# An edge sort moved out of its own stage into a slot pipeline with the convolution, and edge counts made two columns at a time

## The reference

```python
x = x + _L0_conv_ref(_ln_c(x), ...)
t = _to_tokens(x)
t = t + _L0_ffn_ref(_ln_t(t), ...)                 # routed experts
x = _from_tokens(t, x)
x = x + _L1_conv_ref(_ln_c(x), L1_conv_weight, L1_conv_bias)   # relu(conv3x3 + bias)
t = _to_tokens(x)
t = t + _L1_ffn_ref(_ln_t(t), ..., L1_ffn_edge_index)
...
# in _L1_ffn_ref
src = jnp.concatenate([edge_index[0], loops])
dst = jnp.concatenate([edge_index[1], loops])
e = jax.nn.leaky_relu(a_src[src] + a_dst[dst], negative_slope=0.2)
e_max = jax.ops.segment_max(e, dst, num_segments=M)
ee = jnp.exp(e - e_max[dst])
denom = jax.ops.segment_sum(ee, dst, num_segments=M)
agg = jax.ops.segment_sum(h[src] * (ee / denom[dst])[:, :, None], dst, num_segments=M)
```

## Time and profile before

| | us |
|---|---|
| median of 3 runs | 11703.05 (11698.67 to 11715.26) |
| the profiled execution, its own time | 11711.42 |
| its span, first to last instruction | 11709.7 |
| sort, 0 to 1040 | 1040 |
| involution and routing, to 3513.5 | 2473.5 |
| experts and node ranges, to 4387.5 | 874 |
| combine and convolution, to 5783 | 1395.5 |
| edge states, join, gates and output | 5927 |

### The profile page before, as it was taken

How to read it: one execution, slowest core, us unless ns; L and a number is a source line. 1 busy time by engine, 2 the same in 40 slices (tenths; PEclk the granted TensorE clock), 3 DMA queues, 4 the chain that set the end, 5 groups by cost and what they waited for, 6 DMA issues and landing times. The chain is left out here.

```text
span 11709.7 us, 84534 instructions
## 1 busy us (share of the span) xinstructions
PE 5363.1 (46%) x20795; PEld 3127.3 (27%) x20795; DVE 4831.0 (41%) x13362; ACT 2011.8 (17%) x3739; POOL 5292.8 (45%) x5293
## 2 busy tenths in 40 slices
PE   0112999999978996888512112121212122121135
PEld 0111666666656772333200000000000000000012
DVE  9996666666657873434211111111111111111168
ACT  0000333333322321111011111111111111111100
POOL 0000111111110004333477777777777777777662
PEclk9755999999989998888756555565556565565568
DMA  0002000000002112332411111111111111111165
GB/s 14 0 0 101 23 23 23 22 21 21 20 19 89 57 52 51 56 58 59 51 34 36 33 36 35 35 39 31 39 32 39 33 36 34 36 39 31 39 168 190
DMA packets 382082, 514.68 MB, mean 44 GB/s; under 512 B 215894, under 2 KB 302735, under 8 KB 357139
## 3 DMA queue, kind: packets, MB, share of 16 engines
q1 hardware_dynamic: 184466, 260.41, 7.9%
q0 software_dynamic: 164992, 77.85, 6.8%
q10 hardware_dynamic: 32256, 171.98, 3.7%
HBM read 249.78 MB, written 263.86 MB: 44 GB/s over the span
## 5 line engine op out<-in xcount | busy, mean ns | idle before, releaser
L1501 POOL DMA_INDIRECT e_row<-rows_dram,e_idx x4096 | 4031.5, 984 | 1264.4 <-issue 1264.4
L1447 PE MATMUL e_bank<-e_hid,e_w 128*128 128x512 f32 x1024 | 592.9, 714 | 4189.1 <-ACT e_hid L1477 4189.1
L1534 DVE COPY e_idx<-e_allidx 128x64 int32 x64 | 13.2, 206 | 4353.4 <-DMA e_row<-rows_dram,e_idx 4353.4
L1447 PEld LDWEIGHTS e_bank<-e_hid,e_w 128*128 128x128 f32 x1024 | 220.7, 223 | 4492.4 <-issue 4492.4
L388 POOL COPY a_xc<-a_xp 128x1573 f32<-128x1573 f32 x104 | 167.7, 1617 | 1224.2 <-PE a_bank L441 1111.7
L205 DVE TENSOR_SCALAR a_cnta_hot<-a_cnta_iota,a_cnta_part 128x256 bf16<-128x256 bf16 x2368 | 693.1, 293 | 0.0
L1485 ACT ACTIVATE e_ex<-e_dx 128x512 f32<-128x512 f32 x64 | 40.3, 630 | 3573.7 <-DVEq L1547 3573.7
L204 DVE TENSOR_SCALAR a_cnta_hot<-a_cnta_iota,a_cnta_part 128x128 bf16<-128x128 bf16 x2368 | 649.6, 274 | 0.0
L397 POOL DMA_INDIRECT xb_dram<-a_so,a_sidx x256 | 251.4, 982 | 813.5 <-DVE a_sidx L664 548.1
L467 PE MATMUL a_bank<-a_taps,a_xt 121*128 121x100 f32 x2704 | 590.9, 360 | 2.0 <-ACT a_xt L531 2.0
L951 POOL DMA_INDIRECT v_dram<-c_td,c_fidx x256 | 251.4, 982 | 736.4 <-DVE c_td L1076 660.8
(11 more groups left out here) (345 smaller groups left out, 10655.0 us busy)
## 6 DMA issues: line engine op xcount, KB each, us to landing
e_row<-rows_dram,e_idx POOLq DMA_INDIRECT x4096
ys_dram<-e_y ACTq DMA_DIRECT2D x64, 1024.0 KB, 4.0
f_ye<-ys_dram SPq DMA_DIRECT2D x64, 1024.0 KB, 4.8
res_dram<-e_st ACTq DMA_DIRECT2D x64, 768.0 KB, 3.3
xb_dram<-a_taps SPq DMA_DIRECT2D x4, 5120.0 KB, 31.1
b_tok<-xb_dram SPq DMA_DIRECT2D x80, 256.0 KB, 2.7
yb_dram<-b_y ACTq DMA_DIRECT2D x80, 256.0 KB, 2.0
x_dram<-a_xs SPq DMA_DIRECT2D x9, 2048.0 KB, 6.3
```

The lines of the kernel that those rows point to most:

```text
L1447: mm = nc.tensor.matmul(bank[UPB + n % DNB][:], w2[:, n % NE, f], hid[:, n % 2, f], start=(f == 0), stop=(f == NF1 - 1))
L1501: nc.gpsimd.indirect_dma_start(row[:, s, u], None, rows, bass.IndirectOffsetOnAxis(ap=idx[:, s, u:u + 1], axis=0)).then_inc(gath[s], 16)
```

## The change

- `sort_edges` and `combine_and_conv` are gone. One stage `combine_conv_sort` takes the place of the latter and does the work of both. The program now begins with `involution_and_routing`. The semaphores cleared between stages are that stage's.
- The new stage is written out (no loop) as 84 slots, from -10 to 73. In slot g each engine does the pieces that fall on g: strip s of image i is convolved in slot 8i + s, added to the image in the next; its cleaning lies ten slots ahead of the image's slot 0, its second layer norm runs from slot 6 to 15, and the table from 13 to 16. So pieces of three images share a slot.
- In every slot DVE also does sort steps, up to 12.5 us by a table of costs, and a turn ends a slot. The sort's last step is in slot 64. In the slot after a turn step, PE begins with the 32 transpositions, and ACT alone copies all eight banks, through a ring of two PSUM banks (`misc`).
- Layer norm there: one matmul with `ident - 1/128` gives the centred strip at once; ACT copies it out and squares it from PSUM. The transposition of the expert results and their addition to the image are one group of matmuls (the image times identity, and four products with identity), copied by ACT. The table's copies are ACT's too.
- Cleaning is in quarters of an image (1024 columns), with one gather buffer. Two image buffers.
- `EdgeCount`: DVE makes two columns at a time with `tensor_tensor` of 256 and 512 bf16 elements, an iota of which each value stands twice against the two columns' parts broadcast in pairs. The one-hot matrices interleave the two columns, so that PE reads every second element. The rings are 9 and 20 pairs.

```diff
 class EdgeCount:
+        self.RING, self.BLK = ring, 2
...
-        self.part = sb(f"{tag}_part", [P, 2, columns], F32)
+        self.part = sb(f"{tag}_part", [P, 2, columns], BF16)
...
-        self.iota = sb(f"{tag}_iota", [P, NHI], BF16)
-        self.hot = sb(f"{tag}_hot", [P, self.RING, P + NHI], BF16)
+        self.iota = sb(f"{tag}_iota", [P, NHI, self.BLK], BF16)
+        self.hot = sb(f"{tag}_hot", [P, self.RING, P + NHI, self.BLK], BF16)
...
     def make(self, dve, i, k):
...
-            h = self.hot[:, c % self.RING]
-            self.nc.vector.tensor_scalar(h[:, 0:P], self.iota[:, 0:P], self.part[:, 0, c:c + 1], None, ALU.is_equal)
-            self.nc.vector.tensor_scalar(h[:, P:], self.iota[:], self.part[:, 1, c:c + 1], None,
+            h = self.hot[:, blk % self.RING]
+            low, high = (self.part[:, d, c:c + self.BLK].unsqueeze(1) for d in range(2))
+            self.nc.vector.tensor_tensor(h[:, 0:P], self.iota[:, 0:P], low.broadcast_to([P, P, self.BLK]),
+                                         ALU.is_equal)
+            self.nc.vector.tensor_tensor(h[:, P:], self.iota[:], high.broadcast_to([P, NHI, self.BLK]),
                                          ALU.is_equal).then_inc(self.hot_ready, 1)
...
     def count(self, pe, i, k):
...
-            h = self.hot[:, c % self.RING]
+            h = self.hot[:, blk % self.RING, :, z]
...
+        clean_at = lambda g: at(g, -10, PAIRS)
+        add_at = lambda g: at(g, -8, PAIRS)
+        centre_c_at = lambda g: at(g, -7, PAIRS)
...
+        norm_c_at = lambda g: at(g, -1, PAIRS)
+        conv_at = lambda g: at(g, 0, LT)
+        out_at = lambda g: at(g, 1, LT)
+        centre_t_at = lambda g: at(g, 6, PAIRS)
...
+        COST = {"sign": 2.4, "rows": 4.6, "both": 5.0, "turn": 0.1}
...
+            for g in range(FIRST, LAST + 1):
+                for t in turn_slot.get(g, ()):
+                    turn(t)
+                if norm_c_at(g):
+                    factors(*norm_c_at(g), rstd_c, rstdc, normed_c, factor_c)
+                if norm_t_at(g):
+                    factors(*norm_t_at(g), rstd_t, rstdt, normed_t, factor_t)
+                if add_at(g):
+                    add(*add_at(g))
...
+                    pe.wait_ge(normed_c, LT * i + min(s + 2, LT))
+                    if n >= 2:
+                        pe.wait_ge(relu_ready, n - 1)
+                    for k in range(K3 * K3):
...
+                        mm = nc.tensor.matmul(convb[n % 2][:], w9[:, k], xp[:, i % 2, 8 * s + a:8 * s + a + 8, b:b + W],
...
+                if out_at(g):
+                    i, s = out_at(g)
+                    n = LT * i + s
+                    dve.wait_ge(relu_ready, n + 1)
+                    nc.vector.tensor_tensor(xs[:, i % 2, strip(s)], xs[:, i % 2, strip(s)], rl[:, n % 2],
+                                            ALU.add).then_inc(x3_ready, 1)
...
+                for z, step in enumerate(steps):
+                    if slot_of[z] == g:
+                        sort_step(*step)
...
-        sort_sems = sort_edges(nc, w["src"], w["dst"], srcs, dsts, cont, ident)
...
-        combine_and_conv(nc, passed, x1, yb, x3, hn, rows, adst, v, first_i, (slots, gates0), ln, ident,
-                         w["conv"])
+        combine_conv_sort(nc, x1, yb, x3, hn, rows, adst, v, first_i, (slots, gates0), ln, ident, w["conv"],
+                          (w["src"], w["dst"], srcs, dsts, cont))
```

More of the change, by code:

```diff
@@ L1147, in _, with take @@
+            pool.wait_ge(gathered, 16 * TILES * B)
+            for z in range(2):
+                pool.wait_ge(spread_out[z], 16 * TILES * B // 2)
         @block.tensor
         def _(pe):
-            for t, (back, a) in enumerate(turns):
+            freed = {"pm": [], "misc": []}
+            def take(ring, sem_, value):
+                n = len(freed[ring])
+                if n >= 2:
+                    pe.wait_ge(*freed[ring][n - 2])
+                freed[ring].append((sem_, value))
+                return (pm if ring == "pm" else misc)[n % 2]
@@ L1150, in _, with turn @@
+            def turn(t):
+                back, a = turns[t]
                 pe.wait_ge(turn_in, t + 1)
                 for q in range(NTURN):
-                    if t:
-                        pe.wait_ge((turn_act, turn_dve)[q % 2], (NTURN // 2) * (t - 1) + q // 2 + 1)
+                    bank = take("misc", turn_act, NTURN * t + q + 1)
                     for z in range(4):
@@ new lines, in centre, with var @@
+            def centre(i, q, ready, sem_, emptied):
+                for c in range(HALF * q, HALF * (q + 1)):
+                    if ready is not None:
+                        pe.wait_ge(ready, LT * i + c + 1)
+                    bank = take("pm", emptied, LT * i + c + 1)
+                    nc.tensor.matmul(bank[:], cmat[:], xs[:, i % 2, strip(c)], start=True, stop=True).then_inc(sem_, 1)
+            def var(i, q, squared, sq, dev, pv, sem_):
+                if q == 0 and i:
+                    pe.wait_ge(dev, i)
+                for c in range(HALF * q, HALF * (q + 1)):
+                    pe.wait_ge(squared, LT * i + c + 1)
+                    nc.tensor.matmul(pv[0:LT, :], ln.pick[:, c], sq[:, c % 2], start=(c == 0),
+                                     stop=(c == LT - 1)).then_inc(sem_, 1)
@@ new lines, in centred @@
+            def centred(i, q, psum, xc, shape, sq, squared, var_):
+                for c in range(HALF * q, HALF * (q + 1)):
+                    act.wait_ge(psum, LT * i + c + 1)
+                    b = bank("pm")
+                    nc.scalar.activation(xc(c), shape(b[:]), ACT.Copy)
+                    if LT * i + c >= 2:
+                        act.wait_ge(var_, LT * i + c - 1)
+                    nc.scalar.activation(sq[:, c % 2], b[:], ACT.Square).then_inc(squared, 1)
+            act.wait_ge(setup, 6)
@@ L1994, in _ @@
             def _(sp):
-                for handle in sort_sems:
+                for handle in routing_sems:
                     sp.sem_clear(handle)
-        involution_and_routing(nc, passed, x, x1, xb, (slots, gates0), (w["dst"], counts), ln, ident, w["involution"])
         experts(nc, passed, xb, yb, v, (w["dst"], counts), ident, w["experts"])
```

694 lines of the change are left out of this document (398 added, 296 removed).

## The result

The changed kernel takes 10861.15 us (median of 4 runs, 10848.47 to 10865.63), the kernel before 11709.15 beside it. The ratio is 0.9277, 95% interval 0.9262 to 0.9292: 848 us less. The forecast was 10825; the time is 36 above it and inside the range.

What follows compares the result with a forecast made beforehand. No engine bounds the whole; DVE bounds the sort, and neither PE nor DVE fills the convolution stage. 11711.4 - 1038 + 3 + 237 - 81 = 10832 profiled, 10825 as median; range 10730 to 11200.

Steps and rivals of the forecast that it cites:

- The front: Sort stage ahead of the others: leaves the front, -1038 us; more semaphores cleared between stages, +3.
- The new stage: Combine, convolution and sort stage: 1632 us along DVE, replacing 1395.5, so +237 beside the sort's removal.
- The waits around turns: New stage, 14 turns: 86 us waiting for PE's work left in the slot, 99 for the turns themselves.
- Other slots and the clock: New stage: 14 us where other slots have more PE than DVE work, 30 for PE's slow clock starts.
- What is left: New stage's end: 22 us for layer norm and table of the last image, 48 for its 32 scatters.
- PE's sum: New stage: PE works 1156 us of 1632, with 498 for the convolution, so it is not the bound.
- The edge counts: Involution stage: a DVE column at 0.28 us instead of 0.36 ends PE's waits, -81 us; experts nothing.
- rival 4: Counting matmuls: interleaved one-hot matrices make weight loads 0.19 instead of 0.10, +369 less slack, 11190 us; chance 0.08.
- 1, the clock: New stage: PE at 1.2 GHz for a fifth more of its work, +115 us, 10940; chance 0.15.
- 2, serialised slots: New stage: PE waits for banks `pm` behind DVE's sort steps, losing the overlap, +190 us, 11015; chance 0.08.
- 3: Edge counts: `tensor_tensor` at one element a cycle, +284 us in place of -81, experts +40, 11230; chance 0.10.
- 5: New stage: PE at 1.2 GHz throughout, stage 2592 us, whole 11783, slower than before; chance 0.03.

Runs made afterwards that it cites:

- the runs with the parts apart: Kernel before with only the new edge counts: 11636.7 us, ratio 0.9950; changed kernel with the old edge counts: 10920.8 us, ratio 0.9336.
- column_by_column: Changed kernel with a pair's one-hot matrices one behind the other, the comparison going through one column, then the other: 11342.4 us, ratio 0.9693.

## Why the prediction was right, and where it was off

**The front.** The sort's stage of its own is gone, and what comes ahead of the new stage shows nothing of it. Right.

**The new stage: 1619 for 1632.** The step was right, term by term:

- DVE's work 1281.1 for 1283. Start 51.2 for 50.
- The waits around turns 175 for 86 + 99 = 185. That this is so near is in part luck: the first kind was 99 for 86, the second 76 for 99. A turn takes 7.35 on average, not 8.5: 6.0 to 6.6 in the one direction and 8.1 to 9.8 in the other.
- Other slots and the clock 31 for 14 + 30. The granted clock was 0.85, as forecast. Most of the 30 for it was not needed.
- What is left, 1619.1 - 1281.1 - 51.2 - 205.5 = 81, stands for 70: the scatters of the last image and some small waits (5.1 for the store of the keys is the largest).

PE's sum was 1156, and it is 1172.8: the convolution took 521.7 and not 498. 23 of its 1152 instructions are over 0.95 us long, most of them 1.06, where it was 3 in the kernel before; 0.59 is the usual length. That fits the lower clock and makes some 10 of the 24 us; what makes the rest was not settled.

**POOL** was sized at 655 and is busy for 741 in DMAs alone, with 156 between them. It is no bound, as said, but the 0.98 for each did not hold beside the sort (below).

**The edge counts: -50 for -81. This is the step that failed,** and it was the reading of a wait. DVE's rate was right (0.53 for 0.56), "DVE ahead of PE" came true, and "what PE waited goes" as well. But the 80.8 of the earlier trace rows is not what PE lost. The list of that tile in the trace of the kernel before says who waited:

```profile
  PEld a_bank L212: 79.0, 296
...
  PE a_bank L212: 1.9, 12
```

79.0 of it are weight loads, which run ahead of the matmul before them. A load that waits 0.27 beside a running matmul costs only what lasts beyond it. What it cost can be read from the starts of the matmuls. The 296 behind a waiting load began on the mean 0.32 after the one before them, the other directly following ones 0.11: that makes the waits worth 61.

A second term was put at nothing in the forecast: the interleaved matrices cost PE something, though far less than rival 4 feared. Counting matmuls in a row, in the experts stage of the kernel before, of the changed kernel, and of column_by_column, where PE reads neighbouring elements:

```profile
3614.22 2.56 PE L212 MATMUL b_bank<-b_cntb_hot 128*128 128x256 bf16 x22
...
2526.25 2.66 PE L208 MATMUL b_bank<-b_cntb_hot 128*128 128x256 bf16 x22
...
2924.12 2.13 PE L208 MATMUL b_bank<-b_cntb_hot 128*128 128x256 bf16 x18
```

Less the last one's 0.27 they start every 0.109, 0.114 and 0.109. In the involution stage the 1808 matmuls that directly follow another pay 8 us for it, and 61 less 8 is 53. The groups by line say the same: the matmuls were idle for 16.3 (1.9 with a named releaser) and busy for 401.6, and are now idle for 0.0 and busy for 364.4, 53.5 less. The images are 8 x 6.9 = 55 shorter, and the runs with the parts apart give 54 and 57.5. "In the experts nothing" was right (875.6 for 874).

**The sum.** The profiled execution took 10865.6, and the forecast for it was 10832. By stages it lies above the forecast by 29.5 in the involution stage and what stood ahead of it, by 1.6 in the experts and by 15.4 in the rest, and below it by 12.9 in the new stage. The rest is the edge stage and what follows it: 5927 in the one trace of the kernel before, 5932 to 5945 in the nine traces of the changed kernel and of runs on like chips, the gathers' mean 986 to 989 ns for 984. Those nine have the new stage, the new counts or both, and neither part alone is needed for it. Whether the one trace lay low, or how the tiles lie in memory does it, was not settled.

**The rivals.** 1, the clock: 0.85 in the stage, no. 2, serialised slots: the multiplications waited 92 in all, 74 of it at turns, so the ring `pm` costs little. 3: 0.53 a pair; the price was real, though: column_by_column, at 0.93, is 486 slower than the changed kernel, and the rival had 11230 - 10825 = 405. 4: a counting matmul's weight load has a median of 97 ns, before 98, and a matmul starts 0.005 later, at most 20 us over all 4096 where the rival had 369. 5 is excluded by the clock. The Trainium skill's warning in "TensorE: Matmul & The Clock Gate", HAM oscillation, hardly came to bear where PE's work was dense: between 3700 and 4600 PE sat idle for over 0.5 us 29 times, up to 9.2 us, and kept a granted clock of 0.92, 0.95 and 0.93 in the three windows of 300 us. In the 400 us ahead of it, where PE is busy for 162, the clock was 0.69.

## What to carry to other kernels

Laying a DVE stage between the pieces of a PE stage gave nearly what the sum of DVE's work said; what is lost on top is decided slot by slot, so give each slot a quota by the work that stands in it: that gave 88 us more. A wait that the profile shows at a weight load is not all lost to the matmuls (61 of 79 us here); read the matmuls' own idle and busy time, or their starts. And see how the operands of a fast comparison lie, since 0.53, 0.93 and 3.39 us were paid for the same elements.

## What the runs showed of the hardware

**A vector instruction's rate by its layout.** One comparison of bf16 tensors, 256 + 512 elements a partition: 0.53 us with all operands in neighbouring pairs; 0.93 with one operand repeated by a step of 0; 3.39 with each written element 768 bytes from the one before. The Trainium skill, "VectorE: DVE Perf Modes", The perf-mode tier table, gives `tensor_tensor` in bf16 two elements a cycle. The first agrees: 256 elements more cost it 0.13 (0.33 less 0.20), half of the 0.27 (0.60 less 0.33) that the second pays. For the last it has no figure.

**DVE and POOL hold each other up, both ways.** Gathers beside the sort, in order of time:

```profile
3449.99 0.95 POOL L1041 DMA_INDIRECT c_yt<-yb_dram,keep_slots  x1 [0.30 <-issue]
3450.05 1.22 DVE L1339 TENSOR_TENSOR c_keys<-c_keys 128x1024 f32<-128x1024 f32 x1
3451.18 1.22 DVE L1338 TENSOR_TENSOR c_keys<-c_keys 128x1024 f32<-128x1024 f32 x1
3451.25 1.97 POOL L1041 DMA_INDIRECT c_yt<-yb_dram,keep_slots  x1 [0.30 <-issue]
```

133 of the 256 gathers take over 1.1 us where 0.95 is usual, 1.97 most often, and 132 of these end some 0.8 us after a DVE instruction has ended (here 3453.22, after 3452.40). The mean is 1495 ns over the 256, 984 where the sort doesn't run beside them. The other way, a comparison takes up to 1.80 us in place of 0.42 when POOL's copy of patches (1.70) begins first. And in column_by_column DVE's comparisons, back to back, kept the copy waiting until they stopped. The Trainium skill, "SBUF — State Buffer", Who interferes with whom, says that a vector instruction with two inputs in SBUF contends with a GpSimd instruction that reads SBUF, and that the one which comes second waits until the first has finished. The 1.8 us agree; the 15.84 are more than one instruction's wait.
